# A third probability buffer and another prologue order in gated cross-attention with experts

## The reference

```python
xn = layer_norm(x, gamma_x, beta_x)            # context, 8 x 375 x 256
ln = layer_norm(latents, gamma_l, beta_l)      # tokens, 8 x 112 x 256, normalized before
q = (ln @ Wq).reshape(b, m, h, d)
kv_x = xn @ Wkv;  kv_l = ln @ Wkv
k_x = rope_rotate_k(k_x)
k = jnp.concatenate([k_x, k_l], axis=2);  v = jnp.concatenate([v_x, v_l], axis=2)
attn = softmax(einsum('bhid,bhjd->bhij', q * scale, k))
out = einsum('bhij,bhjd->bhid', attn, v) -> @ Wo
x = x + tanh(g_xattn) * out
# experts: P = softmax(LN(x) @ Wg), top 2 of 8, renormalized
y = sum_e P_norm[e] * (gelu(LN(x) @ W1[e] + b1[e]) @ W2[e] + b2[e])
x = x + tanh(g_ffn) * y
```

## Time and profile before

| | us |
|---|---|
| median of 3 timed runs | 558.62 |
| lowest and highest | 558.58, 559.13 |
| profiled execution, device time | 560.93 |
| its span | 559.2 |
| PE busy in the span | 455.5 (81%) |
| DVE, ACT, POOL busy | 307.0, 266.9, 194.0 |

### The profile page before, as it was taken

One profiled execution on the slowest core, in us unless ns is written; L12 is line 12 of the kernel. 1 busy time (PEld: TensorE's weight loads), 2 busy tenths in 40 slices (PEclk: granted clock), 3 DMA queues, 4 the chain that ended last, 5 costly groups with the idle time before them and its releaser, 6 DMA issues. The chain is left out here.

```text
span 559.2 us, 9193 instructions
## 1 busy us (share of the span) xinstructions
PE 455.5 (81%) x3173; PEld 379.4 (68%) x3173; DVE 307.0 (55%) x708; ACT 266.9 (48%) x568; POOL 194.0 (35%) x218
## 2 busy tenths in 40 slices
PE   1689797986879868689688766368999999999991
PEld 1578565664656646567565554328999999999991
DVE  4455635245263453625433372355888888888850
ACT  3331255544436455463635621106666766767640
POOL 4031045443634346444353025630222342222322
PEclk9999879797898979889798965557999999999997
DMA  7200000000000009950034001168578777776223
GB/s 220 65 4 25 1 28 2 27 2 2 27 1 28 0 1 291 250 110 1 1 138 164 1 2 55 51 221 253 154 230 254 211 215 214 199 208 189 45 33 85
DMA packets 41863, 56.04 MB, mean 100 GB/s; under 512 B 1745, under 2 KB 37153, under 8 KB 41808
## 3 DMA queue, kind: packets, MB, share of 16 engines
q1 hardware_dynamic: 36848, 49.80, 29.3%
q0 software_dynamic: 4960, 5.72, 6.2%
q10 hardware_dynamic: 16, 0.00, 0.0%
HBM read 40.37 MB, written 16.07 MB: 101 GB/s over the span
## 5 line engine op out<-in xcount | busy, mean ns | idle before, releaser
L1375 POOL DMA_INDIRECT acc_scratch<-yv,xt x28 | 49.0, 1750 | 130.1 <-DVE yv L1528 125.8
L655 ACT ACTIVATE prob<-sc,negmax 112x487 f32<-112x487 f32 x64 | 42.6, 666 | 104.5 <-DVE negmax L862 60.7
L1397 ACT ACTIVATE hf<-ph,b1t 128x256 f32<-128x256 f32 x112 | 47.1, 472 | 47.8 <-PE ph L1603 47.1
L862 DVE TENSOR_REDUCE negmax<-sc 112x1 f32<-112x487 f32 x64 | 39.4, 657 | 51.2 <-PE sc L1111 51.2
L871 DVE TENSOR_TENSOR heads<-out_t,po 128x112 f32<-128x112 f32 x32 | 8.7, 271 | 91.6 <-ACT out_t L671 91.6
L1136 PEld LDWEIGHTS po<-probt,vals 125*64 125x64 f32 (+1 forms) x512 | 29.4, 156 | 28.8 <-issue 16.2
L663 ACT COPY probt<-pt 125x448 f32<-125x448 f32 x64 | 34.7, 545 | 26.4 <-PE pt L1119 26.2
L1111 PE MATMUL sc<-keys,queries 64*112 64x488 f32 x128 | 42.3, 743 | 1.6 <-ACT keys L623 0.7
L1119 PE MATMUL pt<-ident,prob 112*125 112x112 f32 x256 | 41.8, 290 | 0.0
L1119 PEld LDWEIGHTS pt<-ident,prob 112*125 112x125 f32 x256 | 39.0, 208 | 3.0 <-issue 0.3
L1510 DVE TENSOR_TENSOR hl<-hf,hh 128x512 fp32r<-128x512 f32 x56 | 38.8, 693 | 1.9
(11 more groups left out here) (303 smaller groups left out, 1340.4 us busy)
## 6 DMA issues: line engine op xcount, KB each, us to landing
w_first<-in_L_ffn_W SPq DMA_DIRECT2D x10, 1024.0 KB, 9.0
w_next<-in_L_ffn_W SPq DMA_DIRECT2D x10, 1024.0 KB
rows_scratch<-blank SPq DMA_DIRECT2D x2, 4257.0 KB, 32.7
w_third<-in_L_ffn_W SPq DMA_DIRECT2D x8, 1024.0 KB, 8.3
xt<-rows_scratch SPq DMA_DIRECT2D x14, 258.0 KB, 2.8
ctx_t<-in_ctx SPq DMA_DIRECT2D x8, 375.0 KB
w_first<-in_L_xattn_Wkv SPq DMA_DIRECT2D x1, 1024.0 KB, 10.1
x_all<-in_x SPq DMA_DIRECT2D x2, 448.0 KB, 4.3
```

The lines of the kernel that those rows point to most:

```text
L655: act.activation(prob[:, h % 2, 0:JA], sc[h % 2][0:M, 0:JA], ACT.Exp, bias=negmax[:, h % 2:h % 2 + 1], accum_out=total[:, p, h:h + 1]).the ...
L862: dve.tensor_reduce(negmax[:, h % 2:h % 2 + 1], sc[h % 2][0:M, 0:JA], AX, ALU.max, negate=True).then_inc(max_done.sem, 1)
L1375: pool.indirect_dma_start(out=acc_dram, out_offset=bass.IndirectOffsetOnAxis(ap=xt[i % 3][:, n, D + 1:D + 2].bitcast(I32), axis=0), in_=yv ...
L1397: last = act.activation(hf[:, n % 3, u], ph[n % 3][:, u * T:(u + 1) * T], ACT.Gelu, bias=b1t[:, col])
```

## The change

- `prob` gets a third buffer. Even heads use buffer 0, odd heads buffers 1 and 2 in turn (`prob_at`). An even head's exponential still waits for the transposes of head h-2, an odd head's for those of head h-4.
- `affine_rows` is no tensor of its own any more but a corner of `krot`.
- The query weights' low part is subtracted by GpSimd, between its two reciprocal roots; `rope_t` and the gates are loaded behind both.
- VectorE splits half 0 before it normalizes half 1; the key weights' low part comes after the first context's statistics (step 1).
- TensorE turns half 1 behind query group 0, ScalarE makes half 1's high parts ahead of its copy of group 1.

```diff
-        affine_rows = sb("affine_rows", [4 * KD, P])
+        affine_rows = krot[0:4 * KD, 0, 0:P]
-        prob = sb("prob", [M, 2, PP])
+        prob = sb("prob", [M, 3, PP])
+        def prob_at(h):
+            return 0 if h % 2 == 0 else 1 + h // 2 % 2
@@ GpSimd
-            pool.dma_start(rope_t[:], rope).then_inc(small_loaded, 16)
             latent_rstd(0)
+            pool.wait_ge(whi_done, 1)
+            pool.tensor_tensor(deep[1][:, 0:4, :], w2s[:, 0:4, :], deep[0][:, 0:4, :].bitcast(F32),
+                               ALU.subtract).then_inc(wql_done, 1)
+            latent_rstd(1)
+            pool.dma_start(rope_t[:], rope).then_inc(small_loaded, 16)
             for n, g in enumerate((g_xattn, g_ffn)):
                 pool.dma_start(gates[:, n:n + 1], ...)
-            latent_rstd(1)
@@ ScalarE
             keep_queries(0, 0)
+            high_latents(1)
             keep_queries(0, 1)
             high_weights(slice(INNER, 2 * INNER))
-            high_latents(1)
@@ exponent
-                act.wait_ge(ptr_done.sem, ptr_done.at(t, p, h - 1))
-                act.activation(prob[:, h % 2, 0:JA], sc[h % 2][0:M, 0:JA], ACT.Exp,
+                act.wait_ge(ptr_done.sem, ptr_done.at(t, p, h - 3 if h % 2 else h - 1))
+                act.activation(prob[:, prob_at(h), 0:JA], sc[h % 2][0:M, 0:JA], ACT.Exp,
@@ VectorE
                 if b == 0:
+                    dve.wait_ge(wql_done, 1)
                     dve.wait_ge(wvals_done, 1)
             def latents(s):
+                if s == 1:
+                    dve.wait_ge(whi_done, 2)
+                    dve.tensor_tensor(wkvl[:, :, 0:INNER], w1s[:, :, 0:INNER], wkvh[:, :, 0:INNER].bitcast(F32),
+                                      ALU.subtract).then_inc(wkl_done, 1)
+            split_latents(0)
             latent_norm(1)
-            split_latents(0)
-            dve.wait_ge(whi_done, 1)
-            dve.tensor_tensor(deep[1][:, 0:4, :], w2s[:, 0:4, :], deep[0][:, 0:4, :].bitcast(F32),
-                              ALU.subtract).then_inc(wql_done, 1)
             split_latents(1)
-            dve.wait_ge(whi_done, 2)
-            dve.tensor_tensor(wkvl[:, :, 0:INNER], w1s[:, :, 0:INNER], wkvh[:, :, 0:INNER].bitcast(F32),
-                              ALU.subtract).then_inc(wkl_done, 1)
@@ TensorE
             latent_queries(0, 0)
-            latent_queries(0, 1)
             turn_latents(1)
-            for n in range(2, 2 * HP):
+            for n in range(1, 2 * HP):
@@ transpose_probs
-                                        prob[:, h % 2, j * JR:(j + 1) * JR], ident[0:M, 0:M])
+                                        prob[:, prob_at(h), j * JR:(j + 1) * JR], ident[0:M, 0:M])
```

More of the change, by code:

```diff
@@ L1031, in _ @@
             pe.wait_ge(affine_loaded, 4 * 16)
-            pe.transpose(po[:, 0:4 * KD], affine_rows[:], ident[0:4 * KD, 0:4 * KD]).then_inc(affine_tr, 1)
+            pe.transpose(po[:, 0:4 * KD], affine_rows, ident[0:4 * KD, 0:4 * KD]).then_inc(affine_tr, 1)
             turn_latents(0)
             latent_queries(0, 0)
-            latent_queries(0, 1)
             turn_latents(1)
-            for n in range(2, 2 * HP):
+            for n in range(1, 2 * HP):
                 latent_queries(n // HP, n % HP)
```

## The result

The kernel after takes 501.5 us (median of 4 runs, 500.76 to 502.87), the kernel before 558.6 (4 runs). The ratio is 0.898, with a 95% interval of 0.896 to 0.900: 57 us less. Its profiled execution took 500.76 us with a span of 499.0. The two traces lie further apart than the medians, by 60.2 us of span: the profiled run of the kernel before was 2.3 us slower than its median, that of the kernel after 0.7 us faster.

What follows compares the result with a forecast made beforehand. The prediction took the chain behind exp(5)'s wait for transposes, and the slow clock after 4.8 us of TensorE idleness, to set the period. 560.93 less 51.0 and 4.5 is 505.4; timed runs being 2.3 lower, forecast 503, range 496 to 521.

Steps and rivals of the forecast that it cites:

- The wait is the cause: Attention loop: odd exponentials' wait for transposes sets the period through a chain over engines; rival that it isn't: 554 us, chance 0.02.
- loop and tail: Batches b0 to b7: 38.0 us from b1 to b5, 5 each from b0 and b6, 3 from b7; 51.0 in all.
- the prologue: Before the loop: less VectorE work ahead of the first product and a new order; 4.5 us, bounds 2.5 and 6.5.
- The walk: One period followed with b1's durations: 1.5 + 3.7 + 2.4 = 7.6 us less per batch, period 26.9.
- the clock: TensorE after its 4.8 us of idleness: clock 1.00 instead of 0.50; 2.4 us a batch, range 0 to 3.0.
- The projection: Output projection, behind exp(3), out_t and heads: starts 1.5 us sooner per batch.
- b0, b6, b7: The first and the last two batches: gains of 5, 5 and 3 us, the last with bounds 1 and 3.7.
- the power on GpSimd: Prologue, 13.1 to 14.1: holds back VectorE's two subtractions, first product at 15.3 us; without it 14.3 and 1 us less.
- Behind the first product: Prologue: queries end near 28.1, context's transposes come at 29.4 instead of 33.94; the 4.5 us shift is kept.
- The new wait in the old one's place: Rival: variance chain meets every rotation step, context's transposes idle 4 us, clock falls; period about 31, 526 us; chance 0.13.
- the first rival: The clock falls all the same, so its terms are lost: 519 us; chance 0.15.
- the slower one: Rival: TensorE sits at 1.2 GHz for most of a batch; 588 us with half of it low; chance 0.02.

Runs made afterwards that it cites:

- old_wait: Kernel after, three buffers kept, but every exponential waits again for the transposes of head h-2; 552.8 us.
- only_h3: Kernel after, but only head 3's exponential is let go early; those of heads 1, 5 and 7 wait for the transposes of head h-2; 541.6 us.
- filler_short: Kernel before, all waits kept, with 9 and 10 unread identity products in TensorE's gaps before the last key and the context's transposes; 557.5 us, ratio 0.996.
- only_h5: Kernel after, but only head 5's exponential is let go early; those of heads 1, 3 and 7 wait for the transposes of head h-2; 523.9 us.
- rope_first: Kernel after, with the load of rope_t moved back to the front of GpSimd's queue; 501.3 us.
- buffer_alone: Kernel before with only the third buffer, the later wait and affine_rows in krot; old prologue; 506.9 us, ratio 0.905.

## Why the prediction was right

- **The wait is the cause.** Right. The exponential's wait for T(h-2) held out_t, heads, output rstd, rotation and keys one behind another. old_wait puts 51.3 us on it, where the sum had 51.0 for loop and tail.
- **How near the number is.** The 503 lie 1.5 from the 501.5 measured, and part of that is luck. By the traces the loop and tail gained 54.4 us where the sum had 51.0, and the prologue 5.8 where it had 4.5: 60.2 for 55.5. The 2.3 us taken off because the timed runs were faster than the profiled one made up half of this.
- **The walk.** Per batch of b1 to b5 the forecast was 5.2 us of idleness and 2.4 of clock, period 26.9. Measured: idleness went from 6.6 to 1.1, so 5.5, the period from 34.5 to 26.5, so 8.0, which leaves 2.5 for the clock. From exp(4) to the context's transposes the walk had 10.6 us (117.78 to 128.4); the trace has 10.5. The order in which the waits end, norm last, was right. It left 1.3 us of idleness before the context's transposes; 0.95 is there.
- **The projection.** Forecast 1.5 us from exp(3); only_h3 gained 11.2 us, 1.6 in each of batches 1 to 5 at a clock that stayed at 0.89 to 0.90. In batch 6 it gained twice that, since the clock rose there too, which the sum didn't give to this exponential.
- **b0, b6, b7.** 5, 5 and 3 forecast; 5.6, 5.3 and 3.4 found.
- **The clock.** The size was right by the sum, but the picture was loose. I gave it as a term that stands beside the waits, to be had by closing the 4.8 us of idleness, and argued that the lone gap of 1.78 is harmless. filler_short and only_h5 show that it isn't: with the large gap closed, the small one takes the dip in most batches. The whole term comes only with the last large gap. It was right for the change because this leaves none above 1.03 us in batches 0 to 6.
- **The prologue.** The mis-sized term: 4.5 forecast, 5.8 found, within its bounds. The step that failed is the power on GpSimd holding VectorE's subtractions for 1 us; the first product came at 14.40, near the lower bound of 14.3, and not at 15.3. rope_first and the kernel after show the overlap with no hold. The Trainium skill, page "SBUF — State Buffer", section "SBUF: two separate sides", would have GpSimd's instruction keep VectorE out for its whole length; these rows don't bear this out for a power of 4 columns, though the rotation's 512 columns did so in the earlier trace rows. That row was misread besides: its 2.44 us cover two multiplications of the rotation (1.29 and 1.26 us from 125.03 to 127.54) and not one, so a meeting in the loop would have cost more than the one step of 1.3 us that the walk gave it. The other way round it held: crstd took 1.78 us instead of 0.86 beside VectorE's subtraction. The weights also came 0.6 us sooner without rope_t ahead of them, which I had left out; it gave 0.3 us on the first product.
- **Behind the first product.** The 0.9 us were not simply kept. TensorE ended the queries at 27.98, with 28.1 forecast. Its first products of 448 columns start every 0.37 us and the later ones every 0.21; the slow stretch lasts 5.8 us here and lasted 4.6 before, which the sum left out. The context's transposes then waited 0.50 us and not 1.3, so they came 0.9 ahead of the forecast all the same. Another 0.3 us are gained between them and T(0) of batch 0.
- **The rivals.** The new wait in the old one's place was real in kind (the normalized context) but 0.95 us long and not 4, because the variance chain ended just as the rotation began. Their starts are 0.01 to 0.14 us apart in batches 1 to 5 and the walk had them meet, so that it came out this way is in part luck. The clock at 1.00 rules out the first rival and the slower one.
- **SP and the DMAs.** The blank rows and expert weights had to go out in shorter batches; no wait for the experts' weights shows in the trace after, and the one for the rows of b1 is 5.5 us where it was 5.4.

## What to carry to other kernels

When one kind of wait is named often on an engine that isn't the bottleneck, list what is queued behind it on that engine and follow it through the others; here one buffer of 2 KB per partition was worth 9% because three later hand-overs hung on it. Walk one period with the durations of the trace, and count a TensorE clock below full speed as part of the gap's price, to be had back in full only when no gap of that size is left. Before splitting an effect into terms, run parts alone and together: 11 and 29 us alone were 47 together, and the busy time of TensorE says why.

## What the runs showed of the hardware

- TensorE's clock fell to its lower level (1.2 of 2.4 GHz) behind single gaps of 1.78 and 1.84 us: the projection took 3.2 to 3.5 us instead of 1.98 in batch 1 of filler_short and batch 2 of only_h5. In batch 1 of only_h5 and at most projections of the kernel before, the same gap left it alone. What decides between them wasn't found.
- The kernels whose loop has such dips scatter more on one chip: 557.1 to 561.9 us for the kernel before and 551.7 to 557.1 for old_wait, against 505.8 to 507.5 for buffer_alone beside them. That the dips' places cause the scatter isn't shown, and it isn't general: only_h3 (clock 0.89 to 0.90 in the loop) spans 2.2 us and filler_short (0.96) 1.9, the kernel after 2.1.
- GpSimd's power on 112x4 elements (1.02 us) ran beside a two-input VectorE subtraction without holding it, in rope_first and in the kernel after; a VectorE subtraction of 1.22 us ahead of GpSimd's power on 125x3 stretched that from 0.86 to 1.78.
- A product of two fp32 128x128 operands shows as two TensorE instructions and 0.23 us in all.
- The profile's granted clock reads 1.00 in the kernel after from 14.4 to 20 us, while the products of 448 columns start every 0.37 us; from 20.4 us on they start every 0.21. The kernel before has the same from 17.6 to 22.2. There the pace of the products tells more than the column does.
